# Cross-attention block: key weight on ACT's queue, projection weight converted amid the queries, second tile's exponentials in one piece

## The reference

```
xq  = layer_norm(x, qn_w, qn_b);  ctx = layer_norm(context, cn_w, cn_b)
q   = xq @ q_w;  k, v = split(ctx @ kv_w)            # 16 heads of 32
att = softmax(where(mask, -FLT_MAX, q @ k^T * 32**-0.5))
x   = x + (att @ v) @ proj_w + proj_b
h   = layer_norm(x, n2_w, n2_b)
out = x + gelu(h @ fc1_w + fc1_b) @ fc2_w + fc2_b     # 512 -> 2048 -> 512
```

## Time and profile before

| | us |
|---|---|
| median of 3 runs | 1130.79 (1130.38 to 1131.98) |
| the profiled execution | 1135.25 |
| its span, first to last instruction | 1133.5 |
| TensorE busy | 1110.7 (98%) |
| VectorE busy | 575.0 (51%) |
| ScalarE busy | 408.0 (36%) |
| GpSimd busy | 234.1 (21%) |

### The profile page before, as it was taken

How to read it: one execution, slowest core, us unless ns; L and a number is a source line. 1 busy time by engine, 2 the same in 40 slices (tenths; PEclk the granted TensorE clock), 3 DMA queues, 4 the chain that set the end, 5 groups by cost and what they waited for, 6 DMA issues and landing times.

```text
span 1133.5 us, 16436 instructions
## 1 busy us (share of the span) xinstructions
PE 1110.7 (98%) x5857; PEld 944.7 (83%) x5857; DVE 575.0 (51%) x1152; ACT 408.0 (36%) x1193; POOL 234.1 (21%) x186
## 2 busy tenths in 40 slices
PE   7799999999999999999999999999999999999998
PEld 6599989999999888888888888888888888888887
DVE  6778878887898755632423323322332332232212
ACT  3656655666667644412211311221221131121110
POOL 3333355335554420100100100100110110010000
PEclk8999999999999999999999999999999999999999
DMA  7011111131110034202002002002001001100101
GB/s 246 13 31 58 38 38 56 57 117 42 57 59 20 29 113 139 66 15 70 1 1 75 1 2 75 1 0 75 1 1 72 4 1 38 38 1 1 38 1 38
DMA packets 40193, 48.77 MB, mean 43 GB/s; under 512 B 11013, under 2 KB 19245, under 8 KB 40135
## 3 DMA queue, kind: packets, MB, share of 16 engines
q1 hardware_dynamic: 39503, 46.89, 12.5%
q10 hardware_dynamic: 632, 1.06, 0.3%
HBM read 30.54 MB, written 16.78 MB: 42 GB/s over the span
## 4 chain that ended last, share of the span: by engine, by line
PE 81%; DVE 13%; ACT 3%; issue 2%; DMA 1%; DVEq 0%; SPq 0%; ACTq 0%
PE bank L1422 31%; PE bank L1393 31%; PE bank L1292 8%; PE bank L1250 4%; PE bank L1231 3%; DVE nmax L893 2%; DVE PTl L916 2%; ACT S L675 1%; DVE bnst L940 1%; DVE xhat L952 1%; PE bank L1405 1%; DVE xTl L899 1%; DVE S L886 1%; DVE qTl L905 1%; DMA kvw<-in_L_xattn_kv_w 1%
## 5 line engine op out<-in xcount | busy, mean ns | idle before, releaser
L1422 PE MATMUL bank<-w,gTh 128*128 128x512 f32 x1024 | 319.2, 393 | 0.0
L1132 DVE CAST gTh<-g 128x512 fp32r<-128x512 f32 x128 | 56.9, 445 | 443.0 <-ACT g L796 443.0
L796 ACT ACTIVATE g<-bank,cols 128x512 f32<-128x512 f32 x128 | 88.2, 689 | 471.6 <-PE bank L1393 470.1
L1422 PEld LDWEIGHTS bank<-w,gTh 128*128 128x128 f32 x1024 | 192.4, 188 | 42.6
L1422 PE MATMUL bank<-w,gTl 128*128 128x512 f32 x512 | 200.4, 391 | 0.0
L1393 PE MATMUL bank<-hT0h,w 128*128 128x512 f32 x512 | 162.3, 398 | 0.4 <-DVE w L1089 0.4
L1393 PE MATMUL bank<-hT1h,w 128*128 128x512 f32 x512 | 159.2, 392 | 0.1
L486 POOL TENSOR_TENSOR hrs<-hve,mhalf 128x1 f32<-128x1 f32 x32 | 17.6, 551 | 551.7 <-DVE hve L1106 551.7
L1422 PEld LDWEIGHTS bank<-w,gTl 128*128 128x128 f32 x512 | 96.1, 188 | 22.0
L1393 PEld LDWEIGHTS bank<-hT0h,w 128*128 128x128 f32 x512 | 94.7, 188 | 22.2 <-DVE w L1089 0.6
L1393 PEld LDWEIGHTS bank<-hT1h,w 128*128 128x128 f32 x512 | 95.1, 188 | 20.2 <-issue 0.9
(11 more groups left out here) (108 smaller groups left out, 1804.2 us busy)
## 6 DMA issues: line engine op xcount, KB each, us to landing
xr<-in_x SPq DMA_DIRECT2D x16, 512.0 KB, 3.5
x_scratch<-xr SPq DMA_DIRECT2D x16, 512.0 KB, 2.8
x<-x_scratch SPq DMA_DIRECT2D x8, 1024.0 KB, 5.6
out<-x SPq DMA_DIRECT2D x7, 1024.0 KB, 4.3
w1raw<-in_L_xattn_fc_w SPq DMA_DIRECT2D x16, 256.0 KB, 2.9
w2raw<-in_L_xattn_fc_w SPq DMA_DIRECT2D x16, 256.0 KB, 2.7
kvw<-in_L_xattn_kv_w SPq DMA_DIRECT2D x2, 1024.0 KB, 11.6
qraw<-in_L_xattn_q_w ACTq DMA_DIRECT2D x4, 256.0 KB, 8.2
```

The lines of the kernel that those rows point to most:

```text
L796: act.activation(g[:, :], bF[j % 2][:, :], ACT.Gelu, bias=cols[:, F1B + j:F1B + j + 1]).then_inc(a_gelu.sem, 1)
L1132: dve.tensor_copy(gT[HI][j % 4][:, :], g[:, :]).then_inc(v_ghi.sem, 1)
L1422: mm = pe.matmul(bC[t][:, :], gT[d][j % 4][:, t * P:(t + 1) * P], w2[:, j, w, :], start=(j == 0 and i == 0), stop=(j == JT - 1 and i == 2))
```

## The change

On SP's queue, the four DMAs of `q_w` take the place of the key half of `kv_w`, and unit 1's input goes ahead of the two masks. On ACT's queue the key half takes the place of the four. In `prep="q"` the four casts of the projection weight stand ahead of the first query half on ScalarE, and their four low halves ahead of it on VectorE; statistics and variance of unit 2 stand between the two low query halves; the low halves of the query weight come behind unit 0's x-hat, and GpSimd zeroes both value tiles at once. In `prep="scores"`, tile 1 is done as in the loop (`less_max`, `exp_all`, `exp_sum`), x-hat of unit 2 is made ahead of tile 1's masked scores, and the first low query half ahead of the sum. The two semaphores that were advanced by one at the start in place of these steps are now advanced by the steps themselves.

```diff
--- before.py
+++ after.py
@@ -379,10 +379,11 @@
         load_x(static(0))
         for i in range(3):
             load_row(sp, i)
-        sp.dma_start(kvw[:, :, 0:C], kv_w[:, 0:C].rearrange("(k p) n -> p k n", p=P)).then_inc(d_kw, 16)
+        for kk in range(KT):
+            sp.dma_start(qraw[:, kk, :], q_w.rearrange("(k p) n -> k p n", p=P)[kk]).then_inc(d_qk[kk], 16)
+        load_x(static(1))
         load_mask(static(0))
         load_mask(static(1))
-        load_x(static(1))
         sp.dma_start(kvw[:, :, C:2 * C], kv_w[:, C:2 * C].rearrange("(k p) n -> p k n", p=P)).then_inc(d_vw, 16)
         sp.wait_ge(d_x[0], 16)
         load_x(static(2))
@@ -530,16 +531,17 @@
             if prep == "q":
                 v_xhat.wait(pool, k.plus(2), UT - 1)
                 zero_values(0)
+                zero_values(1)
                 may_negate(k.plus(2))
                 negative(k.plus(2))
                 x_rstd()
-                v_xhat.wait(pool, k.plus(3), UT - 1)
-                zero_values(1)
                 return
             if prep == "scores":
                 may_negate(k.plus(2))
                 negative(k.plus(2))
                 x_rstd()
+                v_max.wait(pool, k.plus(1), 1)
+                less_max(1).then_inc(p_less.sem, 1)
                 probs(0)
                 probs(1)
                 pool.wait_ge(d_projb, 16)
@@ -593,8 +595,7 @@
 
         for i in range(3, 7):
             load_row(act, i)
-        for kk in range(KT):
-            act.dma_start(qraw[:, kk, :], q_w.rearrange("(k p) n -> k p n", p=P)[kk]).then_inc(d_qk[kk], 16)
+        act.dma_start(kvw[:, :, 0:C], kv_w[:, 0:C].rearrange("(k p) n -> p k n", p=P)).then_inc(d_kw, 16)
         def keys_hi(h2):
             act.wait_ge(t_keys, h2 + 1)
             if h2 == 0:
@@ -688,8 +689,8 @@
             if prep == "q":
                 act.wait_ge(v_wscale, 1)
                 wq_hi(0)
+                ctxT_half()
                 wq_hi(1)
-                ctxT_half()
                 wq_hi(2)
                 wq_hi(3)
                 x_hi(0)
@@ -697,21 +698,19 @@
                 keys_hi(0)
                 keys_hi(1)
                 q_row()
+                for c in range(KT):
+                    wp_hi(c)
                 act.wait_ge(v_qbias, 1)
                 q_hi(0)
-                wp_hi(0)
-                wp_hi(1)
                 q_hi(1)
-                wp_hi(2)
-                wp_hi(3)
                 return
             if prep == "scores":
                 x_hi(0)
                 x_hi(1)
                 exps(0, 0, H)
                 values_hi(0)
-                exps(1, 0, H)
                 q_hi(0)
+                exp_all(1)
                 q_hi(1)
                 values_hi(1)
                 return
@@ -808,8 +807,6 @@
     def vector_program(dve):
         for c in counts1:
             dve.sem_inc(c.sem, c.start)
-        dve.sem_inc(v_esum.sem, 1)
-        dve.sem_inc(p_less.sem, 1)
         dve.memset(f32(kbd[HI][:, :, :, :]).rearrange("p a b c -> p (a b c)"), 0.0).then_inc(v_zero, 1)
 
         def ctx_stats():
@@ -927,10 +924,10 @@
                                   ALU.add).then_inc(v_esum.sem, 1)
 
             def recip(t):
-                if t == 1 and prep is None:
+                if t == 1:
                     v_esum.wait(dve, s, 0)
                 else:
-                    a_exp.wait(dve, s, t)
+                    a_exp.wait(dve, s, 0)
                 dve.reciprocal(rsum[:, s.u, t, :], esum[:, s.u, t, :]).then_inc(v_rsum.sem, 1)
 
             def stats(tiles=range(UT)):
@@ -970,11 +967,11 @@
                 variance()
                 return
             if prep == "q":
-                wq_lo(0)
                 ctxT_half()
                 n = f
                 normed()
                 n = k.plus(3)
+                wq_lo(0)
                 wq_lo(1)
                 wq_lo(2)
                 wq_lo(3)
@@ -987,7 +984,12 @@
                 normed()
                 keys_lo(1)
                 q_bias()
+                proj_weights(range(KT))
                 q_lo(0)
+                n = k.plus(4)
+                stats()
+                v_bn.wait(dve, n, UT - 1)
+                variance()
                 q_lo(1)
                 return
             if prep == "scores":
@@ -996,19 +998,15 @@
                 maximum(0)
                 x_lo(0)
                 x_lo(1)
+                normed()
                 for g_ in range(KT):
                     masked(1, g_)
                 maximum(1)
                 recip(0)
-                stats()
-                v_bn.wait(dve, n, UT - 1)
-                variance()
                 values_lo(0)
-                proj_weights(range(2))
+                q_lo(0)
+                exp_sum()
                 recip(1)
-                proj_weights(range(2, KT))
-                normed()
-                q_lo(0)
                 q_lo(1)
                 values_lo(1)
                 return
```

## The result

The changed kernel takes 1123.1 us (median of 5 runs, 1122.9 to 1125.5) against 1130.79 (1130.33 to 1133.21): the ratio is 0.9933, 95% interval 0.9918 to 0.9949. That is 7.7 us less; the forecast was 1122.9, 7.9 less. The profiled execution took 1124.4 us, its span 1122.6.

The account below looks back on a forecast made before the run. TensorE, busy 98% of the span, was taken as the bound, with gains only in its waits and low-clock stretches. Terms 6.1 + 1.8 + 0 = 7.9 us off 1130.8 gave 1122.9 us; 8-in-10 range 1118.5 to 1126.8.

Parts of the forecast that it names:

- The loads: DMA queues at the start: swapping key half and query weight gains nothing, keys start at 13.5 us.
- The queries of unit 0: Preparation, 27 to 34 us: second low query half, and TensorE behind it, come 1.01 us later, bounds 0.6 and 1.6.
- The scores stage: Preparation, 34 to 55 us: unit 0's first score at 49.1 instead of 55.20, gain 6.1 us.
- The clock: Unit 0's step: low clock behind the gap goes, saving 2.26 us, less 0.5 given back: 1.8 us.
- the 0.5 over 22.72: Unit 0's step: charge for the values' second low half now ahead of masked scores on VectorE; at most 0.68.
- The rest moves as a whole: Loop: what is taken out ahead of unit 1's first score at 80.18 moves the whole rest forward.
- the late chain: Rival, scores stage: GpSimd and VectorE hinder each other, first score at 52.6, gain 4.4, time 1126.4 us; chance 0.15.
- the ratio of 2.75: Late-chain rival: two conversions took 3.52 us beside GpSimd against 1.28 without; at that ratio the exponentials' sum takes 2.5 more.
- The early key: Rival, loads: keys start at 11.7 instead of 13.54, gain 11.7, time 1119.1 us; chance 0.11.
- The projection weight: Rival, unit 0's queries: late landing of this weight delays them; landing at 36 gives 1133.8 us; chance 0.07.
- the slope: Projection-weight rival: from a landing at 25.1 us each microsecond later delays queries and TensorE by one.

Follow-up runs that it names:

- both experiments: Changed kernel with its DMAs issued as before the change: 1123.35 us; kernel before with only the changed kernel's DMA order: 1131.75 us against 1131.44.
- the second trace: The changed kernel run once more, unaltered, for another trace: 1123.60 us against 1131.80 for the kernel before, ratio 0.9933.
- the wide filler: Kernel before plus 8 unused matmuls of 512 columns in TensorE's idle time ahead of unit 0's first score: 1129.55 us against 1131.69.
- the bolder order: Changed kernel with two projection-weight low halves ahead of each query half, statistics behind second maximum, x-hat behind last query half: 1123.87 us against 1131.80 before.

## Why the prediction was right

**The loads** (0, 1.3 us of scatter unforeseen). Right for the time, by both experiments, to within 1 us. Where the keys start was wrong: the sum had 13.5, the changed kernel has 12.23 and 12.42, and before 12.5 I had called it a sign of being wrong in the loads. The other sign, casts of `praw` that wait for a DMA, came up as well, in the second trace. Neither sign was good for its purpose, since with the old loads the keys start at 12.51 to 12.90 too. What the term had to hold was the scatter between executions, which moved the keys from 12.15 to 13.54; that the sum was of differences within one trace, and not of places, is why it did no harm.

**The queries of unit 0** (1.01 us later). The wait for the second query half grew by a little: 0.99 at 31.12, and 0.48 at the first. The halves are 2.46 us apart (27.65 to 30.11), where the sum had 2.49. Measured from the copy of the query bias, the transpose behind the second half came 32.84 - 27.62 = 5.22 us later in the kernel before and comes 31.12 - 25.05 = 6.07 us later in the changed one. That is 0.85 us more, within the bounds of 0.6 to 1.6.

**The scores stage** (first score 6.1 sooner). From that transpose to the first score 15.23 us, by the sum 49.1 - 33.85 = 15.25; before 22.36. The change of that stretch is 7.13, less the 0.85 of the step above: 6.3, forecast 6.1. The sum had the chain level with TensorE's own work. In truth TensorE set the start, with the chain 0.4 us ahead (0.58 less the 0.14 of a hand-over); the reason is in the overlap of operations that I had added end to end. The product that reads the value copies, at 55.40, has no wait ahead of it.

**The clock** (1.8). The step of unit 0 took 23.23 us, forecast 23.2. But the 0.5 over 22.72 is not what I charged it for, the values' low half in front of the masked scores. Some 0.3 of it is the first score's own record, 0.70 us right behind the values' products and 0.41 or 0.44 behind a wait: the moved conversions alone and the wide filler have 22.92 and 22.93 with the same low half in front. The other 0.2 no run separates. The wide filler measured the low clock apart: 2.05 us, against the 2.26 charged, and 1.5 to 2.1 over all traces with the gap. That the clock would stay whole was argued from idle times (1.67 left, half of the 3.25 with the low clock behind it); it came true, in the changed kernel with 0.99 us, but the argument was no rule: in the kernel with the loads alone the keys start at the half clock behind 1.24 us. There was luck in that.

**The rest moves as a whole.** 1053.0 us from unit 1's first score to the end in the changed kernel, 1053.3 before.

The rivals: the late chain did not occur. The contention it was built on is real: 4.44 for 1.28 us in the kernel with the exponential alone, 3.40 for 1.00 in the bolder order. But it does not meet every operation: in the changed kernel the sum ran in 1.44 us from 43.35 to 44.79, partly beside GpSimd's first product, which ended near 44.25, and in the kernel with the exponential alone, beside the products from 42.43, it took 1.42. The Trainium skill, GPSIMD Engine Reference, in its table of specifications, has VectorE contend with GpSimd for SBUF when it works in a mode with two ports or reads two inputs from SBUF. The traces agree for the conversions, which read two tiles of SBUF, and for the sum, which reads one; x-hat reads one and suffers all the same (0.54 us each in the changed kernel, 3.40 for two beside GpSimd), and whether it is in such a mode no run here shows. With that rule the ratio of 2.75 would not have been put on the sum. The early key did not occur as described: it had the keys at 11.7, and they start at 12.2 to 12.4, with no gain in the time. The projection weight landed 10.4 + 11.0 = 21.4 us after the start. In the first trace its casts from 22.26 to 24.4 waited for nothing; in the second, with everything 1.3 us sooner, they waited 0.51. There a landing 1.8 us later, near 23.3, would have begun to delay VectorE's query half, an estimate (0.36 + 26.34 - 24.93), so in such an execution the slope starts sooner than at 25.1. Beyond it nothing was tried. Its issue on SP's queue and its way from issue to landing (before: the earlier trace rows):

```profile
10.38 0.47 SPq L390 DMA_DIRECT2D praw<-in_L_xattn_proj_w  x1
```

```profile
DMA to landing us min/median/max: 11.0/11.0/11.0
```

One part of the reasoning failed in an experiment. My expectation for the exponential alone was 1 us and it gave nothing, since what it freed went to contention; the forecast of the whole did not depend on it.

## What to carry to other kernels

Ask of a long idle time what the clock does behind it, and charge both: here 6 us of waiting and 2 of half clock. Before two profiles are subtracted, look where each stands in the spread of its own runs: a 3 us piece of their difference was, nearly all of it, the execution's and not the change's. And if a chain has two parts, try each alone: one was worth 6.0 us alone, the other nothing until the first was gone.

## What the runs showed that was not expected

Twenty more instructions in TensorE's program, in idle time, cost 5 to 7 us some 600 microseconds later: a stall of 1.7 to 2.5 us at the start of the second and of the third pass of the loop over blocks, half clock behind the second, and 1059.7 us instead of 1053.3 from unit 1's first score to the end (1139.1 - 79.44). Eight or five more brought no stall. That it is how the loop's instructions come to lie or are fetched is a guess; no run moved the code without adding to it.

The clock does not follow from the length of the last idle time alone. Behind waits of 2.14 and 2.25 us the keys started at the full clock (exponential alone, 20 narrow matmuls), behind 1.24 and 1.97 at the half (loads alone, first trace of the changed kernel). And the fall need not come at the gap: behind 2.10 us (20 narrow matmuls) the first scores still ran at the full clock and the transposes, from 0.95 us behind the first of them, at the half. In the network phase, with TensorE busy up to them, it stayed whole behind stalls of 1.73 and 2.01 us and fell behind those of 2.24 and 2.53.
